# Transformer block with linear attention and eight experts on one core: opening reordered, first transposes moved between the thirds of the running products, expert rows stored by partition with four output buffers

## The chip, the cores and the metric

The kernel runs on one core of one Trainium2 chip, in one launch. A core has a matrix engine (TensorE, PE in the rows), a vector engine (VectorE, DVE), a scalar engine (ScalarE, ACT), a general engine (GpSimd, POOL), a queue engine (SyncE, SP) and 16 DMA engines that all queues share. Each engine executes its own instruction stream in order and waits on semaphores; nothing but these waits ties the engines together. The metric is the device time of one execution in microseconds (us), as the median of three runs.

## The reference

Sixteen sequences of 256 tokens with 128 features (4096 tokens) go through one adaptive-norm block: linear attention with running sums, then a mixture of 8 experts of which each token takes 2.

```python
h = layernorm(x) * (1 + ca) + sa                  # ca, sa, ga, ...: rows made from L0_c @ L0_wmod
q, k, v = split(h @ qkv_w.T + qkv_b)              # 16 heads of 8
q, k = relu(q) + 1e-6, relu(k) + 1e-6
kv    = cumsum(einsum('bhld,bhle->bhlde', k, v), axis=2)
num   = einsum('bhld,bhlde->bhle', q, kv)
den   = maximum(einsum('bhld,bhld->bhl', q, cumsum(k)), 1e-6)
x = x + ga * ((num / den) @ out_w.T + out_b)
h = layernorm(x) * (1 + cb) + sb
# experts: u = rmsnorm(h @ W_in.T); logits = u @ Wr.T; the best 2 of 8 by logits + bias
# oe = rmsnorm((silu(u @ Wg[e].T) * (u @ Wu[e].T)) @ Wd[e].T); out = sum of gates * oe
x = x + gb * (rmsnorm(out) @ W_out.T)
```

## The kernel before

Tokens lie on the 128 partitions, so a sequence ("batch" in the code, `b`) is two tiles (`NT = 2`). The whole program is written out by hand: five functions, one for each engine, each with its own list of instructions and `wait_ge` calls. What stands first in a function is executed first; there is no scheduler. Five stretches follow each other.

**Opening (0 to about 20 us).** SP issues the loads one behind the other on one queue (L385 to L403): modulation weights, the first two batches of `x`, the key/value bias, constants (`cst`), small weights (`small`), output bias `bo`, expert bias, `place`, and the other 14 batches of `x`. The five loads from `cst` to `place` count on one semaphore, `w_ld`, and DVE, POOL and PE wait for all five (`16 * 5`). Then SP waits for `gate_row`, stores it to HBM, reads it back broadcast as `gates_bc` (2 MB), and issues the gate/up weights `wgu` (4 MB), the down weights `wd` (2 MB) and the rest. On POOL the key/value bias is cut into three bf16 parts (L464 to L475), then the gated output bias in the same way (L477 to L483); ACT copies these parts (L573) before its first norm. DVE prepares small weights (L808 to L821) before its first statistics (L829).

**Attention steps (about 17 to 210 us).** `pipelined(eng, step)` calls `step(nrm, qkv, att, prj, inp, rte)` on each engine: in step `s` batch `s` is normalised, batch `s-1` gets q, k and v, batch `s-2` its running sums, `s-3` the output projection, `s-4` the input projection of the experts and `s-5` the routing. Steps 0 to 7 are written out, steps 8 to 15 are a hardware loop of two steps in a pass, steps 16 to 20 are written out again. Within a step:

- POOL forms the products k x v (`kv`, L499, two of 128x1024) once ACT has `k`, and scatters routed rows to HBM (L520).
- PE makes the running sums with a triangular matrix (`running_state`, L1302). For each of the two tiles this is nine matmuls in three thirds (`cc` = 0, 1, 2), each third in a PSUM bank of its own. Before, all three thirds of tile 0 come first in the step, then the transposes of the normalised input (`xn2`, L1347, and `xn`, L1354), the transposes of the reciprocals (L1361), k/v (L1373, L1376), q (L1383), the output projection (L1395, L1398), the thirds of tile 1, and the head sums (L1320 to L1331).
- DVE starts a step with `den` (L1010), multiplies each third by q (L866), and `attnT` (L1035) needs `rdenT` from ACT.
- ACT copies the transposed inputs to `hT` (L610), `h2T` (L616) and `rdenT` (L624), in this order.

Side work is spread over steps: maxima of `wgu` on DVE in steps 2 to 5 (`wmaxs`, L969), squares of `wd` on ACT, one quarter each in steps 4 to 7 (L658), and on POOL the multiplication of `gates_bc` by the output weights (L504, one of 128x2048, in step 2; L511, four of 128x512, one in each of steps 1 to 4).

**Routing tables (210 to 241 us), expert tiles (241 to 415 us).** 39 tiles of 256 rows go through gate, up and down projections; POOL scatters the results to `ybuf` in HBM (L533), two scatters a tile, to the row numbers in `place`.

**End (415 us on).** SP waits for all scatters and loads `ybuf` in four pieces of 2, 2, 4 and 8 batches (`LOADS`, L439). ACT takes the root (`rms_of_rows`, L759), DVE the coefficients (L1200, L1202), POOL multiplies the first expert's rows (`halve`, L547), DVE adds the second (`mix`, L1211), ACT squares, PE transposes and projects (L1530, L1538), DVE adds `x` into an output buffer (`ob`, L1226), and SP stores it (L444). There are two output buffers.

Of the kernel before, what the change touches and what calls it, by code (L numbers as in the profile page):

```python
# [21 lines left out]
ALU = mybir.AluOpType  # L22
ACT = mybir.ActivationFunctionType
AX = mybir.AxisListType

P = 128
# [41 lines left out]
def shape_constants():  # L68
# [14 lines left out]
    token = np.arange(TOK // P)[None, :, None] * P + p[:, None, None]  # L83
    place = (token * K + np.arange(K)).reshape(P, -1).astype(np.uint32)
# [15 lines left out]
def block_kernel(nc, x, c_wmod, weights_all, qkv_b, out_b, e_bias, wguT, wdT, e_norm, consts, place, filler, out):  # L100
    ctx = ExitStack()
    with ctx:
# [114 lines left out]

        spare = prod[0:1].rearrange("o t s -> o (t s)")
# [27 lines left out]
        def in_late(first, n):  # L246
# [18 lines left out]
        half, mix, mixT, ob = (prod[:].rearrange("p t s -> p (t s)")[:, i * 2 * L:(i + 1) * 2 * L].rearrange(  # L265
            "p (j t d) -> p j t d", j=2, t=NT) for i in range(4))
# [13 lines left out]
        LOADS = [(0, 2), (2, 4), (4, 8), (8, B)]  # L280
# [8 lines left out]
        eps_set = sem("eps_set")  # L289
# [22 lines left out]
        scattered, yb_ld, stored = two("scattered"), [sem(f"yb_ld{i}") for i in range(4)], two("stored")  # L312
# [21 lines left out]
        SCALE_STEP = B - WN - 1  # L334
        WO_CHUNKS = 4
# [4 lines left out]
        SQUARE_STEPS = range(B - WN - 4, B - WN)  # L340
# [41 lines left out]
        def _(sp):  # L382
# [16 lines left out]
            sp.dma_start(wgu, wguT).then_inc(wgu_ld, 16)  # L399
# [42 lines left out]
            def store(b, p):  # L442
                sp.wait_ge(ob_done, b + 1)
                sp.dma_start(out[bass.ds(b, 1), :, :].rearrange("o (t p) d -> p (o t) d", p=P),  # L444
                             ob[:, p]).then_inc(stored[p], 16)

            with sp.Fori(0, B // 2) as i:
                for p in range(2):
                    store(2 * i + p, p)
            for p in range(2):  # L450
                sp.wait_ge(stored[p], 16 * (B // 2))
# [3 lines left out]
        def _(pool):  # L455
# [5 lines left out]
            pool.wait_ge(bkv_ld, 16)  # L461
# [1132 lines left out]
```

## Time and profile before

| | us |
|---|---|
| median of 3 runs (lowest, highest) | 454.98 (454.23, 456.43) |
| profiled execution | 456.44 |
| its span in the trace | 454.6 |
| PE, DVE, ACT, POOL busy | 364.9, 337.4, 290.8, 250.6 |

The profiled execution was as long as the longest of the three timed ones; 1.84 us of it lie outside the span. Busy time says little here, since the bound changes from stretch to stretch: between 240 and 410 us PE is busy 166.5 of 170 us, between 120 and 186 us both PE (62.0 of 66) and DVE (58.5) are nearly full, and before 20 us no engine but the DMA is. The rows are read by stretch. In a timeline row the first number is the start from the span's beginning, the second the length from the first to the last instruction of the group, in brackets the idle time of the engine just before it, with what ended it. "issue" means that the trace shows nothing that was waited for.

### The profile page before, as it was taken

The page shows a single profiled execution, that of the slowest core. Times are in us where ns is not written, and L with a number is a line of the kernel's source. Part 1 is how long each engine was busy: PE and PEld are TensorE (multiplying, and loading weights), DVE is VectorE, ACT ScalarE, POOL GpSimd, SP SyncE. Part 2 cuts the span into 40 slices and gives each one's busy share as a digit, 9 for nine tenths or more (in the row PEclk, how much of TensorE's full clock was granted, in tenths as well). Part 3 has the DMA queues.
Part 4 walks back from the last instruction along what each step waited for, and adds up shares of the span by engine and source line. Part 5 has one row for each costly group of instructions (what it writes and reads, how often), then busy time and mean ns, then how long its engine had stood idle before and what let it go on. Part 6 is the DMA issues. An engine that isn't in the chain of part 4 may idle for free.

```text
span 454.6 us, 13206 instructions
## 1 busy us (share of the span) xinstructions
PE 364.9 (80%) x3903; PEld 319.2 (70%) x3904; DVE 337.4 (74%) x1113; ACT 290.8 (64%) x814; POOL 250.6 (55%) x221
## 2 busy tenths in 40 slices
PE   3379999869999999975107999999999999991474
PEld 2158877658888888864105998999999999980353
DVE  3328899657888888867386788789779888790585
ACT  2244687656777777734733778678778778772585
POOL 4359557557777788853630246456546546464331
PEclk9969999998999999997557999999999999996579
DMA  8895000000000000000142122222122222113923
GB/s 238 305 420 218 2 1 25 25 24 20 25 23 28 25 23 23 23 25 25 41 123 68 40 73 65 52 70 64 52 70 64 61 61 71 36 36 89 343 71 92
DMA packets 21907, 35.67 MB, mean 78 GB/s; under 512 B 3827, under 2 KB 17670, under 8 KB 21350
## 3 DMA queue, kind: packets, MB, share of 16 engines
q1 hardware_dynamic: 17206, 25.39, 18.0%
q0 software_dynamic: 4544, 9.39, 6.1%
q10 hardware_dynamic: 128, 0.53, 0.5%
q8 instruction: 15, 0.25, 0.2%
q14 instruction: 14, 0.11, 0.1%
HBM read 23.80 MB, written 13.47 MB: 82 GB/s over the span
## 4 chain that ended last, share of the span: by engine, by line
PE 47%; DVE 22%; issue 13%; DMA 6%; ACT 5%; POOL 4%; DVEq 1%; SPq 1%; another core or an unknown queue 1%; ACTq 0%; POOLq 0%
PE bank L1472 8%; PE bank L1473 7%; PE bank L1474 7%; DVE prod L866 6%; PE bank L1302 4%; PE bank L1489 4%; PE bank L1488 4%; PE bank L1487 4%; PE bank L1458 2%; PE bank L1376 2%; DVE st L829 2%; DVE wmaxs L969 1%; DVE rows L928 1%; DMA out<-prod 1%; DMA place_sb<-place 1%
## 5 line engine op out<-in xcount | busy, mean ns | idle before, releaser
L533 POOL DMA_INDIRECT expert_rows<-late,to_place x78 | 87.5, 1121 | 93.3 <-DVE late L1158 69.7
L499 POOL TENSOR_TENSOR kv<-kv,v 128x1024 f32<-128x1024 f32 x32 | 67.7, 2135 | 40.8 <-ACT kv L634 40.8
L1472 PE MATMUL bank<-late,w_hi 128*128 128x256 f16 x312 | 85.7, 275 | 1.4 <-issue 0.5
L520 POOL DMA_INDIRECT dispatched<-rows,pos x64 | 67.3, 1052 | 34.3 <-issue 17.7
L1473 PE MATMUL bank<-late,w_hi 128*128 128x256 f16 x312 | 85.6, 274 | 0.0
L1474 PE MATMUL bank<-late,w_lo 128*128 128x256 f16 x312 | 85.5, 274 | 0.0
L1302 PE MATMUL bank<-cst,kv 128*128 128x128 f32 x576 | 73.8, 283 | 3.4 <-POOL kv L499 2.5
L1147 DVE SCALAR_TENSOR_TENSOR kv<-bank,uscale,kv 128x512 f32<-128x512 f32 x78 | 58.2, 747 | 21.0 <-ACT kv L714 16.2
L1302 PEld LDWEIGHTS bank<-cst,kv 128*128 128x128 f32 x576 | 69.6, 198 | 4.9 <-POOL kv L499 3.2
L714 ACT ACTIVATE kv<-bank,descale 128x512 f32<-128x512 f32 x78 | 53.5, 685 | 28.3 <-PE bank L1474 27.2
L720 ACT ACTIVATE kv<-kv 128x512 f16<-128x512 f32 x78 | 49.0, 628 | 19.6 <-DVE kv L1147 16.9
L1152 DVE TENSOR_TENSOR kv<-kv 128x512 f16<-128x512 f32 x78 | 53.6, 687 | 6.5 <-issue 3.9
L1487 PE MATMUL bank<-late,kv 128*128 x312 | 54.3, 219 | 0.5 <-DVE kv L1152 0.5
L1488 PE MATMUL bank<-late,kv 128*128 x312 | 54.3, 219 | 0.0
L1489 PE MATMUL bank<-late,kv 128*128 x312 | 54.3, 219 | 0.0
L866 DVE TENSOR_TENSOR prod<-bank,qT 128x384 f32<-128x384 f32 x96 | 50.0, 545 | 5.3 <-PE bank L1302 5.0
L1472 PEld LDWEIGHTS bank<-late,w_hi 128*128 x312 | 30.7, 98 | 6.6 <-issue 3.0
L1474 PEld LDWEIGHTS bank<-late,w_lo 128*128 x312 | 30.7, 99 | 3.7
L1473 PEld LDWEIGHTS bank<-late,w_hi 128*128 x312 | 30.7, 98 | 3.2
L1487 PEld LDWEIGHTS bank<-late,kv 128*128 128x128 f16 x312 | 30.5, 98 | 1.1 <-issue 0.6
L1488 PEld LDWEIGHTS bank<-late,kv 128*128 128x128 f16 x312 | 30.5, 98 | 0.4
L1489 PEld LDWEIGHTS bank<-late,kv 128*128 128x128 f16 x312 | 30.5, 98 | 0.1
(207 smaller groups left out, 790.0 us busy)
## 6 DMA issues: line engine op xcount, KB each, us to landing
late<-dispatched SPq DMA_DIRECT2D x39, 129.0 KB
late<-wguT SPq DMA_DIRECT2D x1, 4096.0 KB, 16.5
late<-expert_rows SPq DMA_DIRECT2D x1, 2064.0 KB, 12.9
gates_bc<-gate_rows SPq DMA_DIRECT2D x1, 2048.0 KB, 6.9
wd<-wdT SPq DMA_DIRECT2D x1, 2048.0 KB, 20.9
out<-prod SPq DMA_DIRECT2D x16, 128.0 KB, 1.8
expert_rows<-late,to_place POOLq DMA_INDIRECT x78
late<-expert_rows SPq DMA_DIRECT2D x2, 516.0 KB, 4.5
```

The lines of the kernel that those rows point to most:

```text
L499: nc.gpsimd.tensor_tensor(kvt[:, 0:HD, :, :], k_in, v_in.to_broadcast([P, HD, H, HD]), ALU.mult).then_inc(kv_done[t], 1)
L520: pool.indirect_dma_start(hbuf, bass.IndirectOffsetOnAxis(ap=pos[:, p, t * K + k:t * K + k + 1], axis=0), rows[:, p, t, k, :], None).then_ ...
L533: pool.indirect_dma_start(ybuf, bass.IndirectOffsetOnAxis(ap=to_place[:, s, r:r + 1], axis=0), yt[:, s, r, :], None).then_inc(y_scat[s], 16)
L866: nc.vector.tensor_tensor(prod[:, t, cc * THIRD * P:(cc + 1) * THIRD * P].rearrange("p (e i) -> p e i", i=P), cum, qT[:, p, t * P:(t + 1) ...
L1147: nc.vector.scalar_tensor_tensor(gu[:, h, :], U[h], uscale[:], sg[:, h, :], ALU.mult, ALU.mult).then_inc(gu_done, 1)
L1302: last = mm(CUM[cc][:, j * P:(j + 1) * P], kv[:, p, t, e * D:(e + 1) * D], tri, start=True, stop=True)
L1472: mm(o, w_hi[:, w], hi, start=True, stop=False)
L1473: mm(o, w_hi[:, w], lo, start=False, stop=False)
L1474: last = mm(o, w_lo[:, w], hi, start=False, stop=True)
L1487: mm(o, gu_hi[:, s % 2, h, g], wd_hi[:, w], start=(f == 0 and r == 0), stop=False)
L1488: mm(o, gu_lo[:, s % 2, h, g], wd_hi[:, w], start=False, stop=False)
L1489: last = mm(o, gu_hi[:, s % 2, h, g], wd_lo[:, w], start=False, stop=(f == FC - 1 and r == RB - 1))
```

## The change

Four groups of edits:

1. **Opening.** `w_ld` counts `cst` and `small` alone (32), `bo` moves to the semaphore of the key/value bias, `ebias` and `place` to that of the last part of `x`. `x` comes in three parts: batches 0 and 1, 2 to 5 (ahead of `ebias` and `place`), 6 to 15 (behind `gates_bc`). `wgu` is issued by ACT behind its first `hT`. DVE does the statistics of batches 0 and 1 and the norm factors of batch 0 first. The first batch takes its k/v bias from the f32 row `bkv` with two one-row f32 matmuls, and does not wait for the bf16 parts. The parts of the gated output bias come behind the first `kv` on POOL, their copies on ACT behind those of batch 1. In step 2 PE does the q, k, v work of batch 1 ahead of the first running sums. POOL's L504 moves out of the steps, to the front of the expert tiles. The squares of `wd` are two quarters each in steps 6 and 7.
2. **Steps.** PE does thirds 0 and 1 of tile 0, then the transposes of the normalised inputs, then third 2.
3. **Expert rows.** `place` numbers the rows by partition: token `n * 128 + p` goes to row pair `p * 32 + n`. Each partition's rows of a load are then contiguous in HBM.
4. **End.** Loads of 1, 3, 4 and 8 batches; the root and the coefficients of the second load come one batch earlier; four output buffers, in the memory of `kv`.

```diff
-    token = np.arange(TOK // P)[None, :, None] * P + p[:, None, None]
-    place = (token * K + np.arange(K)).reshape(P, -1).astype(np.uint32)
+    place = ((p[:, None, None] * (TOK // P) + np.arange(TOK // P)[None, :, None]) * K + np.arange(K)).reshape(
+        P, -1).astype(np.uint32)
...
-        LOADS = [(0, 2), (2, 4), (4, 8), (8, B)]
+        LOADS = [(0, 1), (1, 4), (4, 8), (8, B)]
...
-        SQUARE_STEPS = range(B - WN - 4, B - WN)
+        SQUARE_STEPS = range(B - WN - DN // 2, B - WN)
...
-            sp.dma_start(bo[:], out_b.to_broadcast([P, D])).then_inc(w_ld, 16)
-            sp.dma_start(ebias[:], e_bias.to_broadcast([P, E])).then_inc(w_ld, 16)
-            sp.dma_start(place_sb[:], place).then_inc(w_ld, 16)
-            sp.dma_start(xs[:, 2 * NT:, :], xv[:, 2 * NT:, :]).then_inc(x_rest, 16)
+            sp.dma_start(bo[:], out_b.to_broadcast([P, D])).then_inc(bkv_ld, 16)
+            sp.dma_start(xs[:, 2 * NT:X_MID * NT, :], xv[:, 2 * NT:X_MID * NT, :]).then_inc(x_mid, 16)
+            sp.dma_start(ebias[:], e_bias.to_broadcast([P, E])).then_inc(x_rest, 16)
+            sp.dma_start(place_sb[:], place).then_inc(x_rest, 16)
...
-            sp.dma_start(wgu, wguT).then_inc(wgu_ld, 16)
+            sp.dma_start(xs[:, X_MID * NT:, :], xv[:, X_MID * NT:, :]).then_inc(x_rest, 16)
...
-                sp.dma_start(yb[:, first * NT:end * NT], ybuf[first * L * K:end * L * K, :].rearrange(
-                    "(n p k) w -> p n k w", p=P, k=K)).then_inc(yb_ld[i], 16)
+                sp.dma_start(yb[:, first * NT:end * NT], ybuf[0:TOK * K, :].rearrange(
+                    "(p n k) w -> p n k w", p=P, k=K)[:, first * NT:end * NT]).then_inc(yb_ld[i], 16)
...
-            pool.wait_ge(bkv_ld, 16)
+            pool.wait_ge(bkv_ld, 32)
...
+                    if isinstance(b, int) and b == 0:
+                        out_bias_parts()
...
+                    if isinstance(b, int) and b == 0:
+                        act.dma_start(wgu, wguT).then_inc(wgu_ld, 16)
...
-                if att is not None:
-                    running_state(att, 0, scale)
+                filling = att is not None and first(att[0])
+                if att is not None and not filling:
+                    running_state(att, 0, scale, range(2))
...
                 if inp is not None or qkv is not None:
                     last.then_inc(turn_ps, 1)
+                if att is not None and not filling:
+                    running_state(att, 0, scale, range(2, 3))
...
                     if first(b):
-                        pe.wait_ge(w_ld, 16 * 5)
-                        pe.wait_ge(bias_part, 11)
-                        pe.wait_ge(w_small, 3)
+                        pe.wait_ge(bkv_ld, 32)
+                        for t in range(NT):
+                            mm(KV[:, t * 2 * D:(t + 1) * 2 * D], ones[0:1, :], bkv[0:1, :], start=(t == 0), stop=False)
...
+                if filling:
+                    running_state(att, 0, scale)
...
-                if again(n):
-                    dve.wait_ge(stored[p], 16 * (n - 1))
+                if not (isinstance(b, int) and b < 4):
+                    dve.wait_ge(stored[j % 4], 16 * (i + j // 4))
...
-            coefficients(1)
-            turn_of_batches(0, (2, 3))
+            turn_of_batches(0, (2,))
             coefficients(2)
+            turn_of_batches(0, (3,))
```

PE's list at the opening before, from the modulation matmuls (`sc`, `c_wmod_sb`) to the first running sums (`cst,kv`):

```order
L1265 MATMUL bank<-c_wmod_sb,sc 16x256
L1270 MATMUL bank<-wrn,small 128x8 [waits w_small]
L1354 MATMUL bank<-cst,xn 128x128 [waits xn_done]
L1373 MATMUL bank<-bkv,ones 128x512 [waits bias_part,w_small,w_ld,hT_done]
L1376 MATMUL bank<-small,hT 128x256 x2
L1383 MATMUL bank<-hT,small 128x256
L1302 MATMUL bank<-cst,kv 128x128 [waits gate_done,kv_done_0]
L1302 MATMUL bank<-cst,kv 128x128 x8
L1354 MATMUL bank<-cst,xn 128x128 [waits q_done,xn_done]
```

The same place in the changed kernel, whose line numbers are higher (L1390 is the transpose of `xn`, L1408 the new f32 bias, L1414 the bf16 bias, L1417 and L1424 k/v and q, L1335 the running sums):

```order
L1300 MATMUL bank<-c_wmod_sb,sc 16x256
L1390 MATMUL bank<-cst,xn 128x128 [waits w_ld,xn_done]
L1408 MATMUL bank<-bkv,cst 128x256 [waits bkv_ld,hT_done]
L1417 MATMUL bank<-small,hT 128x256 x2
L1424 MATMUL bank<-hT,small 128x256
L1427 MATMUL bank<-wrn,small 128x8 [waits w_small]
L1390 MATMUL bank<-cst,xn 128x128 [waits q_done,xn_done]
L1414 MATMUL bank<-bkv,ones 128x512 [waits w_small,k_done,bias_part,hT_done]
L1335 MATMUL bank<-cst,kv 128x128 [waits gate_done,kv_done_0]
L1335 MATMUL bank<-cst,kv 128x128 x8
```

The router's matmul (`wrn`) no longer stands ahead of the first transpose, the wait for the bias parts has moved from the first to the second batch, and the running sums that wait for POOL's first `kv` stand behind the whole k, v and q work of the second batch.

PE's list at the start of a step in the loop, before:

```order
L1302 MATMUL bank<-cst,kv 128x128 [waits cum_used_1_0]
L1302 MATMUL bank<-cst,kv 128x128 [waits cum_used_1_1]
L1302 MATMUL bank<-cst,kv 128x128 [waits den_done,cum_used_1_2]
L1302 MATMUL bank<-cst,kv 128x128 x2
L1347 MATMUL bank<-cst,xn 128x128 [waits q_done,xn2_done]
L1354 MATMUL bank<-cst,xn 128x128 [waits q_done,xn_done]
L1354 MATMUL bank<-cst,xn 128x128
L1361 MATMUL bank<-cst,rden 128x128 [waits rden8_done]
L1373 MATMUL bank<-bkv,ones 128x512 [waits k_done,hT_done]
```

The same place in the changed kernel (L1335 the running sums, L1381 and L1390 the transposes, L1399 those of the reciprocals):

```order
L1335 MATMUL bank<-cst,kv 128x128 [waits cum_used_1_0]
L1335 MATMUL bank<-cst,kv 128x128 [waits cum_used_1_1]
L1335 MATMUL bank<-cst,kv 128x128 x2
L1381 MATMUL bank<-cst,xn 128x128 [waits q_done,xn2_done]
L1390 MATMUL bank<-cst,xn 128x128 [waits q_done,xn_done]
L1390 MATMUL bank<-cst,xn 128x128
L1335 MATMUL bank<-cst,kv 128x128 [waits den_done,cum_used_1_2]
L1399 MATMUL bank<-cst,rden 128x128 [waits rden8_done]
L1414 MATMUL bank<-bkv,ones 128x512 [waits k_done,hT_done]
```

The last three of the nine matmuls of tile 0, with their wait for `den`, have moved behind the four transposes. Everything from L1361 on stands as it did.

## Rows read from the trace of the kernel before

**Rows 1.** Busy times by stretch: busy us and (instructions) of each engine, PE clock

```profile
25.00:30.00 5.00, 3.75 (x21) 3.16 (x21) 2.42 (x9) 0.70 (x2) 3.79 (x3) 0.69 0.97 419
120.00:186.00 66.00, 62.01 (x664) 53.34 (x664) 58.48 (x259) 50.63 (x144) 52.77 (x37) 1.00 0.07 24
240.00:410.00 170.00, 166.54 (x2026) 153.14 (x2027) 138.79 (x274) 123.26 (x308) 83.58 (x74) 0.98 0.22 59
```

**Rows 2.** Timeline of the opening, to the start of step 3

```profile
9.48 0.23 DVE L808 TENSOR_SCALAR wrn<-small 128x8 f32<-128x8 f32 x1 [0.81 <-DMA place_sb<-place]
12.12 0.74 POOL L475 TENSOR_TENSOR bkv<-bkv,bkv_part 3x256 bf16<-3x256 bf16 x1
17.23 0.88 ACT L578 ACTIVATE xn<-x_all,nmr,rs 128x128 f32<-128x128 f32 x2 [0.60 <-DVE nmr L846]
20.11 2.08 PE L1376 MATMUL bank<-small,hT 128*128 128x256 f32 x4
23.35 4.21 POOL L499 TENSOR_TENSOR kv<-kv,v 128x1024 f32<-128x1024 f32 x2 [8.05 <-ACT kv L634]
25.53 3.03 PE L1302 MATMUL bank<-cst,kv 128*128 128x128 f32 x18 [2.49 <-POOL kv L499]
35.99 2.33 DVE L969 TENSOR_REDUCE wmaxs<-late 128x1 f32<-128x1024 f32 x2
38.24 0.18 DVE L1010 TENSOR_SCALAR den<-bank 128x32 f32<-128x32 f32 x1
```

**Rows 3.** DMA issues: source and target, queue, count, size, us to landing

```profile
late<-wguT SPq DMA_DIRECT2D x1, 4096.0 KB, 16.5
gates_bc<-gate_rows SPq DMA_DIRECT2D x1, 2048.0 KB, 6.9
small<-weights_all SPq DMA_DIRECT2D x1, 453.5 KB, 5.2
x_all<-x SPq DMA_DIRECT2D x1, 256.0 KB, 3.4
```

**Rows 4.** Timeline of side work in the steps that are written out

```profile
37.66 4.53 POOL L504 TENSOR_TENSOR gates_bc<-gates_bc,woutn 128x2048 f32<-128x2048 f32 x1
77.24 1.04 ACT L658 ACTIVATE w_lo<-wd 128x1024 f16<-128x1024 f32 x1
85.24 0.56 ACT L610 ACTIVATE hT<-bank,mod_cols 128x256 f32<-128x256 f32 x1 [2.90 <-issue]
```

**Rows 5.** Timeline of two steps of the loop, 146 to 160 us, by engine

```profile
146.11 0.42 DVE L1035 TENSOR_TENSOR attnT<-bank,rdenT 128x256 f32<-128x256 f32 x1 [0.66 <-issue]
152.89 2.25 PE L1302 MATMUL bank<-cst,kv 128*128 128x128 f32 x18
154.85 0.29 ACT L603 ACTIVATE sd<-mv,eps_ln 128x2 f32<-128x2 f32 x1
155.71 0.55 DVE L866 TENSOR_TENSOR prod<-bank,qT 128x384 f32<-128x384 f32 x1
155.76 0.56 ACT L610 ACTIVATE hT<-bank,mod_cols 128x256 f32<-128x256 f32 x1 [0.62 <-issue]
156.38 0.38 PE L1373 MATMUL bank<-bkv,ones 3*128 3x512 bf16 x1 [0.58 <-ACT hT L610]
157.09 0.42 DVE L1035 TENSOR_TENSOR attnT<-bank,rdenT 128x256 f32<-128x256 f32 x1 [0.83 <-issue]
159.00 4.23 POOL L499 TENSOR_TENSOR kv<-kv,v 128x1024 f32<-128x1024 f32 x2 [0.98 <-ACT kv L634]
```

**Rows 6.** Timeline of the end, from the loads of the expert rows on

```profile
417.08 2.78 SPq L439 DMA_DIRECT2D late<-expert_rows  x4
421.06 0.31 ACT L759 ACTIVATE rms<-late,eps_rms 128x8 f32<-128x8 f32 x1 [8.08 <-DMA late<-expert_rows]
441.59 0.61 DVE L1226 SCALAR_TENSOR_TENSOR prod<-bank,rinv,x_all 128x128 f32<-128x128 f32 x2 [0.67 <-DMA out<-prod]
451.52 0.61 DVE L1226 SCALAR_TENSOR_TENSOR prod<-bank,rinv,x_all 128x128 f32<-128x128 f32 x2 [0.75 <-DMA out<-prod]
```

More of the change, by code:

```diff
@@ L311, in block_kernel @@
         ln_st, ln2_st = two("ln_st"), sem("ln2_st")
-        scattered, yb_ld, stored = two("scattered"), [sem(f"yb_ld{i}") for i in range(4)], two("stored")
+        scattered, yb_ld, stored = two("scattered"), [sem(f"yb_ld{i}") for i in range(4)], four("stored")
         lr_done, score_done, max_done, idx_done, oh_done = (
@@ L334, in block_kernel @@
         SCALE_STEP = B - WN - 1
+        X_MID = 6
         WO_CHUNKS = 4
@@ L570, in _ @@
             nc.scalar.activation(junk[:, 0:1], eps_ln[:], ACT.Sqrt)
-            act.wait_ge(bo_part, 6)
-            for i in range(3):
-                nc.scalar.activation(bo_ga3[32 * i:32 * i + B, :], bo_ga_part[:, i], ACT.Copy).then_inc(bo_done, 1)
             def norm(b, p, rs_, nmr_, xn_, nm_done, done):
@@ L645, in step @@
                     norm(nrm[0], nrm[1], rs, nmr, xn, ln_nm, xn_done)
+                if qkv is not None and isinstance(qkv[0], int) and qkv[0] == 1:
+                    act.wait_ge(bo_part, 6)
+                    for i in range(3):
+                        nc.scalar.activation(bo_ga3[32 * i:32 * i + B, :], bo_ga_part[:, i],
+                                             ACT.Copy).then_inc(bo_done, 1)
                 if nrm is not None and not isinstance(nrm[0], int):
@@ L1040, in step @@
                     best(rb, rp)
-                if nrm is not None:
+                if nrm is not None and not (isinstance(nb, int) and nb == 0):
                     norm_inv(nb, sd, rs, ln_sd, ln_rs, np_)
@@ L1044, in step @@
                     best_index(rb, rp)
-                if nrm is not None:
+                if nrm is not None and not (isinstance(nb, int) and nb == 0):
                     norm_shift(nb, mv, rs, nmr, ln_rs, ln_nm, np_)
@@ L1233, in _ @@
             mix_experts(*batch_of_turn(0, 0))
+            coefficients(1)
             mix_experts(*batch_of_turn(0, 1))
@@ L1276, in done_by, with running_state @@
                 return min(b, B) if isinstance(b, int) else b
-            def running_state(att, t, scale):
+            def running_state(att, t, scale, chunks=range(3)):
                 b, p, n = att
-                if not scale:
+                if not scale and 0 in chunks:
                     pe.wait_ge(kv_done[t], b + 1)
-                for cc in range(3):
+                for cc in chunks:
                     if t:
@@ L1383, in step @@
                     mm(TB[:, 0:L], wqkv[:, 0:D], hT[:, p, :], start=True, stop=True).then_inc(q_ps, 1)
+                    if first(b):
+                        pe.wait_ge(w_small, 1)
+                        mm(ND[:, 0:E], w_in_rows, wrn[:], start=True, stop=True).then_inc(router_ps, 1)
+                if filling:
+                    running_state(att, 0, scale)
                 if prj is not None:
```

170 lines of the change are left out of this document (97 added, 73 removed).

## The prediction, on record before the result

> **What bounds the kernel now.** I read the busy times by stretch first, then the timeline of each stretch that the change touches, then the list of DMA issues. The reader should see that no single engine is the bound. In the 66 us of loop steps PE is busy 62.0 us and DVE 58.5 [rows 1]; both have short gaps. Over the expert tiles PE is busy 166.5 of 170 us [rows 1]; the change leaves their instructions alone, so these 170 us stay. That leaves three places: the opening, the start of every step, and the end.
>
> In the opening the first normalised input is ready late: DVE waits until 9.48 for the landing of `place`, which it doesn't use there, ACT's first `xn` comes at 17.23, k/v at 20.11, POOL's first `kv` at 23.35, and step 3 starts with `den` at 38.24 [rows 2]. In a loop step (`attnT` at 146.11 and 157.09: 10.98 us) the same gap shows on three engines: ACT idles 0.62 before `hT`, PE 0.58 behind it, DVE 0.83 (0.66 in the step before) ahead of `attnT` [rows 5]. At the end ACT waits for the first expert rows until 421.06, 3.98 us behind the issue, and DVE waits for stores [rows 6].
>
> **Opening, part by part.** `small` lands 5.2 us behind its issue at 2.5, so at 7.7; the first `x` took 3.4 us, so about 4.6 [rows 3]. DVE's statistics of both batches then run 4.7 to 6.2, and ACT's `xn` (0.88, [rows 2]) is done by about 7.8. Two transposes bring 8.5, `hT` 9.1. The two f32 bias matmuls are not in the trace. Each has the shape of the k/v matmuls, of which two (four passes) took 2.08 us [rows 2]: with that, 2.1 us; a bound below is the bf16 form in [rows 5], 0.38. I take 2.1, since an f32 row is nearest to the f32 rows. So k/v ends at 9.2 + 2.1 + 2.1 = 13.4 where it ended at 22.2. POOL is now later: it waits for `bo` too (about 8.1) and ran 8.0 us of bias work from 4.82, of which 1.27 was waiting; so it is free at about 15.0, and `kv` starts at 15.0 where it started at 23.35. That bounds the saving on this chain at 8.3 us. Batch 1 follows on PE: transposes at 16.4, k/v and q done at 21.3, running sums behind them (3.03 and about 2.6, head sums 2.2) to about 29.2. Before, PE was through at 37.6, just ahead of `den` at 38.24 [rows 2]: 8.4 us saved.
>
> What is late next is `wgu`. In step 2 DVE needs it for two maxima of 2.33 us together, just ahead of `den` [rows 2]. It took 16.5 us behind `gates_bc`, 6.9 us [rows 3]. Now ACT issues it at about 9.2, ahead of `gates_bc` (about 12.5). The DMA moved 419 GB/s at 25 to 30 us [rows 1]. Up to 12.5 `wgu` gets about 1.1 of its 4.2 MB. If both then share evenly, `gates_bc` (2.1 MB) lands at about 22.7 and `wgu`, with the last part of `x` beside it, at 28 to 30. If nothing were gained it would be 32.7 as before; alone it would be done at about 20. I take 29: maxima until 31.4, `den` at 31.4 instead of 38.24, so **6.8 us saved** in place of 8.4; bounds 3.1 (landing at 32.7) and 9.5 (PE reaches its higher clock earlier than it did, and `wgu` is there by 26). POOL has `gates_bc` to wait for between `kv` of batch 0 and 1. Queued behind this wait is `kv` of batch 1, which PE needs at 29.2; it would hurt only if `gates_bc` landed later than about 25.8.
>
> The page "DMA: Bandwidth & Descriptors" of the Trainium skill (sections on queues and rings, and on issuing engines) says that an engine takes turns between the queues it has work for, and that issuing from several engines saves issue time only. By that rule the second queue for `wgu` adds no bandwidth, and the landing times are the shared ones of my sum rather than the 20 us; no row before shows two such loads at once.
>
> The bias parts, the f32 row of the first batch, and the output bias copies lie on engines that wait at that time; I cost them at nothing beyond the times above. Squares of `wd`: a quarter costs ACT 1.04 us and 0.19 for its sum [rows 4]. Steps 4 and 5 lose one each; in step 4 it was on the path for about 0.4, in step 5 the maxima on DVE end last. Steps 6 and 7 get 1.23 more each; ACT waited about 0.5 and 0.9 there for DVE, so 0.3 to 0.8 shows. Behind step 6 ACT stood still for 2.90 us with nothing shown [rows 4], which may hide it or not: **-0.3**, bounds -1.5 and +0.5.
>
> POOL's L504 (4.53 us, [rows 4]) now runs at about 241 to 246, where POOL idled until its first scatter at 254.7: nothing. In step 2 it hid behind ACT's k.
>
> The page "SBUF — State Buffer" (on the engine doors) says that VectorE and GpSimd take turns on one port pair for whole instructions, when VectorE reads two operands there or copies in its fast mode. By it DVE's small copy of row numbers would wait for L504 and the first tile of the experts would come about 0.8 us later. The trace doesn't bear this out: L504 ran beside DVE's `den` at 38.24 without delay, though that reads PSUM.
>
> **Loop steps.** A third of `running_state` is three matmuls, 2.25 / 3 = 0.75 us [rows 5]. The transposes come that much earlier. `hT` was issued at 155.76; it can start when ACT is through with `sd`, 154.85 + 0.29 = 155.1. So 0.62 is gained of the 0.75. PE idled 0.58 for it, and that is all PE has to give: from then on PE is the bound of the step. DVE's `attnT` has 0.66 and 0.83 to give. Third 2 comes 0.4 later, at about 155.5; DVE's last product of tile 0 reads it at 155.71 at the earliest: 0.2 to spare. POOL idles 0.98 a step and keeps 0.4. So each full step becomes 10.4 us. Eight loop steps and step 16: 9 x 0.58 = **5.2 us**. Bounds: 0 if third 2 or another wait takes the place, 7.5 if the two-sided gap goes wholly. In steps 3 to 7 `hT` follows right behind `sd` or the maxima bound: nothing.
>
> **End.** First load 264 KB in runs of 2 KB instead of 516 KB in runs of 1 KB: 3.98 us before, 3.4 for 256 KB in the busy opening [rows 3], 1.8 for 128 KB stores. I take 2.7: 1.3 saved (0.6 to 2.1). The second coefficients, needed one batch earlier, cost and save about alike, 0.5 saved. Four buffers take away DVE's waits for stores, 0.67 and 0.75 [rows 6] and one of like size between them, 2.0 together; I take 1.6, since PE and ACT are close behind. Sum **3.4 us**, bounds 1 and 6. The scatters now write 516-byte rows 33 KB apart for neighbouring tokens; only the last one is on the path (2.4 us), and I see no cost.
>
> **Sum.** 6.8 - 0.3 + 5.2 + 3.4 = 15.1 us. Against the profiled execution's 456.44 that is 441.3. The median of the runs is 1.46 below the profiled one, so 439.9; I say **440.0 us**.
>
> **Rivals.**
>
> *`wgu` is no earlier* (0.17). It lands at 32.7 as before, the opening saves 3.1: 443.7 us. For it: the DMA was at its full rate from 16 us on. Against: it was idle or slow from 12 to 16.
>
> *The gap in the loop moves instead of going* (0.13). DVE's third product or POOL's `kv` ends last: no 5.2, 445.2 us. Against: the spare 0.2 and 0.4.
>
> *More than I sum* (0.17). PE's clock rises early in the opening, the 2.90 us standstill of [rows 4] goes, stores and loads at the end gain their upper bounds: 4 to 6 us more, about 435.
>
> *Slower* (0.02). One mechanism: PE, with no idle time left in the loop, is granted its lower level (1.2 GHz). In the 25 to 30 stretch at 0.69 of full speed the same 18 matmuls took 3.03 us instead of 2.25 [rows 1, 2], k/v 2.08; a step of 10.4 us of PE work would take at least 14. From about five such steps on (3.6 us each against 15.1, with the rest kept) the kernel is slower than before; with all eight it takes 469. Against it: 0.98 to 1.00 granted at 94 to 98% busy [rows 1].
>
> My own case has 0.51, with a range of 437 to 443. What a measurement of this kernel can tell from no change is about 0.5%, 2.3 us. Faster by more than that: all of the first four cases but a rest of 0.02 in which several lower bounds meet: 0.96. Same 0.02, slower 0.02. The range for 8 in 10 takes in the first two rivals and part of the third: 435 to 446.
>
> **What would show it.** `xn` of batch 0 near 7 us and k/v by 14; `kv` on POOL near 15; the first maxima waiting for `wgu` and ending near 31; `den` of step 3 near 31.4. In the loop, steps of 10.4 us, no idle of PE ahead of the k/v bias, `attnT` right behind DVE's product. At the end the first root 2.7 us behind the load's issue, and no wait of DVE for a store. Wrong would be: loop steps of 11 us; `den` of step 3 later than 35; PE clock below 0.95 in the loop; expert tiles longer than before.

## The result, and the profile after

The changed kernel takes 439.86 us (median of four runs, 437.86 to 440.80), beside 455.71 for the kernel before (454.23 to 458.97): a ratio of 0.964, interval 0.957 to 0.970. 440.0 was forecast. The profiled execution took 440.27 us, its span 438.4 us, 16.2 less than before; 15.1 were forecast for it.

The span splits as follows (us). The rows of a step are taken from its `den` to the next one's:

| stretch | before | after | difference |
|---|---|---|---|
| start to `den` of step 3 | 38.24 | 28.90 | -9.3 |
| step 3 | 10.32 | 12.62 | +2.3 |
| steps 4, 5, 6 | 32.06 | 31.22 | -0.8 |
| steps 7 and 8 | 28.58 | 25.82 | -2.8 |
| steps 9 to 16 | 87.56 | 83.39 | -4.2 |
| step 17 | 12.05 | 13.19 | +1.1 |
| from there to the loads of the expert rows | 208.27 | 208.39 | +0.1 |
| loads to the end of the span | 37.5 | 34.9 | -2.6 |

The timeline of the opening of the changed kernel, which answers to [rows 2] (start, length, engine, line, in brackets the idle time ahead and what ended it):

```profile
6.48 0.88 ACT L585 ACTIVATE xn<-x_all,nmr,rs 128x128 f32<-128x128 f32 x2 [0.73 <-DVE nmr L830]
9.39 2.07 PE L1408 MATMUL bank<-bkv,cst 1*128 1x256 f32 x4 [0.72 <-ACT hT L617]
11.39 2.07 PE L1417 MATMUL bank<-small,hT 128*128 128x256 f32 x4
15.59 4.20 POOL L506 TENSOR_TENSOR kv<-kv,v 128x1024 f32<-128x1024 f32 x2
20.96 5.18 PE L1335 MATMUL bank<-cst,kv 128*128 128x128 f32 x36
26.01 1.29 POOL L515 TENSOR_TENSOR gates_bc<-gates_bc,small 128x512 f32<-128x512 f32 x1 [3.78 <-DMA gates_bc<-gate_rows]
26.65 2.33 DVE L993 TENSOR_REDUCE wmaxs<-late 128x1 f32<-128x1024 f32 x2
27.24 4.21 POOL L506 TENSOR_TENSOR kv<-kv,v 128x1024 f32<-128x1024 f32 x2
28.90 0.18 DVE L1034 TENSOR_SCALAR den<-bank 128x32 f32<-128x32 f32 x1
29.43 2.56 PE L1335 MATMUL bank<-cst,kv 128*128 128x128 f32 x12 [1.01 <-POOL kv L506]
```

`xn`, k/v (done at 13.5) and POOL's first `kv` (15.59) are where the prediction put them, and the f32 bias row took 2.07 us. The maxima of `wgu` (L993) follow without a wait. POOL is the one that waits: until 26.01 for `gates_bc`, with `kv` of batch 1 queued behind it at 27.24, and PE stands 1.01 us for that. The 12 matmuls behind this wait take 2.56 us; in [rows 5] 18 took 2.25. The DMA issues, against [rows 3]:

```profile
late<-wguT ACTq DMA_DIRECT2D x1, 4096.0 KB, 15.8
gates_bc<-gate_rows SPq DMA_DIRECT2D x1, 2048.0 KB, 15.1
```

`gates_bc` takes 15.1 us instead of 6.9. A step of the loop, against [rows 5], and the end, against [rows 6]:

```profile
131.44 0.83 PE L1335 MATMUL bank<-cst,kv 128*128 128x128 f32 x6
131.58 0.29 ACT L610 ACTIVATE sd<-mv,eps_ln 128x2 f32<-128x2 f32 x1
131.79 0.57 ACT L617 ACTIVATE hT<-bank,mod_cols 128x256 f32<-128x256 f32 x1
132.42 0.39 PE L1414 MATMUL bank<-bkv,ones 3*128 3x512 bf16 x1
133.12 0.42 DVE L1068 TENSOR_TENSOR attnT<-bank,rdenT 128x256 f32<-128x256 f32 x1
...
143.59 0.42 DVE L1068 TENSOR_TENSOR attnT<-bank,rdenT 128x256 f32<-128x256 f32 x1
...
403.53 1.76 SPq L442 DMA_DIRECT2D late<-expert_rows  x4
406.10 0.30 ACT L774 ACTIVATE rms<-late,eps_rms 128x4 f32<-128x4 f32 x1 [6.43 <-DMA late<-expert_rows]
...
435.37 0.61 DVE L1260 SCALAR_TENSOR_TENSOR kv<-bank,rinv,x_all 128x128 f32<-128x128 f32 x2 [0.47 <-PE bank L1584]
```

The third `cc` = 2 (131.44) runs while ACT makes `hT`; none of these rows has a bracket, on any of the three engines; the step is 10.47 us instead of 10.98. At the end the first root comes 2.57 us behind the issue, and no add waits for a store. Busy times in the loop, against [rows 1]:

```profile
120.00:186.00 66.00, 63.42 (x679) 54.92 (x677) 58.62 (x258) 50.73 (x146) 54.83 (x40) 1.00 0.08 27
```

PE is busy 63.4 of 66 us (62.0 before) at a granted clock of 1.00: no sign of the rival in which it falls to its lower level.

One pair of rows was not in the sum. It lies where the experts start; the first row is the copy in the kernel before:

```profile
242.69 0.16 DVE L1140 COPY to_place<-late 128x2 uint32<-128x2 uint32 x1
...
227.73 4.50 POOL L534 TENSOR_TENSOR gates_bc<-gates_bc,woutn 128x2048 f32<-128x2048 f32 x1 [6.66 <-DVE late L1148]
228.35 3.90 DVE L1173 COPY to_place<-late 128x2 uint32<-128x2 uint32 x1
```

DVE's copy of row numbers (two for each partition) takes 3.90 us (before: 0.16). It ends at 232.25, POOL's instruction at 232.23.

### The profile page after: what moved, and what is told of

It is laid out like the page before. It is cut to its first block, busy times and chain, and to the rows that moved or that the text cites. A ratio compares the mean times of both kernels' runs of the same rounds, so it can differ in the third digit from the quotient of the medians.

```text
span 438.4 us, 13203 instructions
## 1 busy us (share of the span) xinstructions
PE 366.1 (84%) x3906; PEld 321.1 (73%) x3907; DVE 338.8 (77%) x1113; ACT 290.9 (66%) x814; POOL 249.9 (57%) x221
## 3 DMA queue, kind: packets, MB, share of 16 engines
HBM read 23.80 MB, written 13.47 MB: 85 GB/s over the span
## 4 chain that ended last, share of the span: by engine, by line
PE 56%; DVE 19%; issue 10%; DMA 7%; ACT 3%; POOL 3%; DVEq 1%; another core or an unknown queue 0%; ACTq 0%; SPq 0%; POOLq 0%
PE bank L1518 8%; PE bank L1520 8%; PE bank L1519 8%; PE bank L1335 6%; DVE prod L890 5%; PE bank L1533 4%; PE bank L1535 4%; PE bank L1534 4%; DMA gates_bc<-gate_rows 3%; PE bank L1504 2%; PE bank L1417 2%; DVE st L813 2%; PE bank L1444 1%; ACT junk L782 1%; DVE x_all L1085 1%
## 5 line engine op out<-in xcount | busy, mean ns | idle before, releaser
L1335 PE MATMUL bank<-cst,kv 128*128 128x128 f32 x576 | 77.0, 286 | 1.2 <-POOL kv L506 1.0
L1335 PEld LDWEIGHTS bank<-cst,kv 128*128 128x128 f32 x576 | 72.0, 201 | 1.9 <-POOL kv L506 1.1
L585 ACT ACTIVATE xn<-x_all,nmr,rs 128x128 f32<-128x128 f32 (+1 forms) x64 | 28.0, 485 | 6.5 <-DVE nmr L830 5.7
L1533 PEld LDWEIGHTS bank<-late,kv 128*128 128x128 f16 x312 | 30.5, 98 | 1.9 <-issue 1.4
L1534 PEld LDWEIGHTS bank<-late,kv 128*128 128x128 f16 x312 | 30.5, 98 | 0.4
## 6 DMA issues: line engine op xcount, KB each, us to landing
late<-wguT ACTq DMA_DIRECT2D x1, 4096.0 KB, 15.8
gates_bc<-gate_rows SPq DMA_DIRECT2D x1, 2048.0 KB, 15.1
```

The costliest lines, as they stand in the source:

```text
L1335: last = mm(CUM[cc][:, j * P:(j + 1) * P], kv[:, p, t, e * D:(e + 1) * D], tri, start=True, stop=True)
L1533: mm(o, gu_hi[:, s % 2, h, g], wd_hi[:, w], start=(f == 0 and r == 0), stop=False)
L1534: mm(o, gu_lo[:, s % 2, h, g], wd_hi[:, w], start=False, stop=False)
```

## Experiments

Twelve more runs were made, in three groups of four; each group had a chip of its own. The kernel before took 456.74 us in the first group, 458.22 in the second and 448.07 in the third, so times are compared within a group and by their ratio to it. `after_again` is the changed kernel as it is, `thirds_only` the kernel before with one edit, `both_pool` the changed kernel with two; the others are the changed kernel with one. The changed kernel itself ran in group 2 only, so in the other two groups its edits are judged by their siblings. A time expected in us was meant for the first chip and isn't to be held against another one: the steps and waits are.

| group | kernel | us | ratio (interval) |
|---|---|---|---|
| 1 | thirds_undone | 445.31 | 0.977 (0.971, 0.983) |
| 1 | wgb_early | 437.69 | 0.958 (0.953, 0.963) |
| 1 | chunk_behind | 434.37 | 0.951 (0.945, 0.957) |
| 1 | written10 | 435.74 | 0.953 (0.947, 0.958) |
| 2 | after_again | 439.02 | 0.962 (0.954, 0.970) |
| 2 | wgu_sp | 439.57 | 0.961 (0.954, 0.969) |
| 2 | squares_old | 440.59 | 0.964 (0.955, 0.972) |
| 2 | by_token | 438.66 | 0.959 (0.949, 0.968) |
| 3 | loads_old | 433.34 | 0.967 (0.964, 0.969) |
| 3 | ob2 | 435.98 | 0.974 (0.970, 0.978) |
| 3 | thirds_only | 441.61 | 0.985 (0.982, 0.989) |
| 3 | both_pool | 430.38 | 0.959 (0.956, 0.962) |

### The transposes between the thirds: undone, and alone

`thirds_undone`:

```diff
-                    running_state(att, 0, scale, range(2))
+                    running_state(att, 0, scale)
...
-                if att is not None and not filling:
-                    running_state(att, 0, scale, range(2, 3))
```

> The changed kernel with all three thirds of tile 0 ahead of the transposes again, in every step but step 2, which stays as changed. My theory (the gap behind the late transposes was PE's own idle time, 0.52 a step): loop steps go from 10.46 back to 10.97 us, PE idles 0.58 ahead of the k/v bias, about 5 us slower over eight loop steps and step 16, and 1 to 2 us more in steps 3 to 7 if the same gap was there: 445 us. Rival (the loop gained from elsewhere, from the moved side work for instance): loop steps stay near 10.5 us and the kernel near 440.

The loop steps are 10.97 us again (10.37 to 10.40 in the three other kernels of the group), and the gap is back as it was. Two rows of its timeline:

```profile
145.28 0.56 ACT L617 ACTIVATE hT<-bank,mod_cols 128x256 f32<-128x256 f32 x1 [0.61 <-issue]
145.90 0.38 PE L1412 MATMUL bank<-bkv,ones 3*128 3x512 bf16 x1 [0.58 <-ACT hT L617]
```

The other way round, `thirds_only` puts the same edit alone into the kernel before.

> The kernel before with the one edit that the transposes stand between the thirds of the running products in steps 3 to 16, all else as before. Theory: loop steps 10.4 to 10.5 us instead of 10.97 as in the changed kernel, and 0.2 to 1.2 us less in steps 3 to 7: 5 to 6 us faster than before, 450 us. It also gives a second trace of steps 7 and 8 of the old kernel (13.47 and 15.11 us in the first): if they are near 13.5 and 13 here, the fast step 8 of the changed kernel is no gain of the change. Rival (the gain in the loop hangs on the other edits, side work among them): 455.

0.985 of 448.07 is 6.6 us less (5.1 to 8.1). Its loop steps are 10.30 us, as in the three changed kernels of its group. Taken away, the edit costs 0.57 to 0.60 us a step on one chip (10.97 against 10.37 to 10.40). Put in alone it leaves the same step as all edits together, and that is 0.67 us below the 10.97 of the first trace; no trace of the kernel before was taken on this chip, so part of the 0.67 can be the chip's. The rival that the gain needs the other edits has fallen. And steps 7 and 8 took 11.13 and 10.54 us in it, with the old opening and the old squares.

### Steps 7 and 8: is the gain there one of the change?

`written10` writes out steps 8 and 9 too, so that the hardware loop begins with step 10.

> The changed kernel with steps 8 and 9 written out too, so that the hardware loop begins with step 10. The two slow steps 7 and 8 (12.2 and 13.6 us from den to den in the changed kernel, 13.5 and 15.1 before; 10.46 in the loop) show ACT, DVE and PE all standing still by issue or remote. Theory A (it comes with entering the loop, the code of its first pass): the slow steps become 9 and 10, steps 7 and 8 take about 10.5. Theory B (it comes with the work of steps 7 and 8, the first scatters among it): they stay 7 and 8. Either way about 440 us.

Step 7 took 12.20 and step 8 12.19 us, step 9 10.14, and the first two of the loop 10.39 and 10.40. Theory A is refuted: the slow steps did not move with the loop. Theory B is not shown by this run alone. The changed kernel a second time:

> The changed kernel once more, for a second trace. In its first trace two written-out steps took longer than in three kernels that keep them as they are: step 8 took 13.58 us (12.30, 12.19 and 11.64 in the others) and the step behind the loop 13.19 (10.97 to 10.99). If these standstills are chance, this trace has them smaller or elsewhere, near 12.2 and 11.0, and the kernel takes 437 to 438.5 in it. If they belong to this kernel, both come back: 13.6, 13.2 and 440.

Step 17 came back at 11.03, step 8 at 12.94, between the two expectations. The place stays, the size varies. Steps 7, 8 and 17, in us:

| | step 7 | step 8 | step 17 |
|---|---|---|---|
| before | 13.47 | 15.11 | 12.05 |
| changed, first trace | 12.24 | 13.58 | 13.19 |
| after_again | 12.44 | 12.94 | 11.03 |
| chunk_behind (group 1) | 12.25 | 12.30 | 10.97 |
| squares_old (group 2) | 13.48 | 13.06 | 11.59 |
| thirds_only, loads_old, ob2, both_pool (group 3) | 11.13 | 10.53 to 10.54 | 10.40 to 10.41 |

In group 3 the standstills are absent in all four kernels, with the old opening or the new. No edit is needed for them to come or go, and the -2.8 and +1.1 us in the first table can't be credited to the change. One thing stays open: where the standstills occur, step 7 took 13.47 and 13.48 us in the two traces with the old squares (before, `squares_old`) and 12.20 to 12.99 in the eight with the new ones, so the place of the squares may have a part in 1 us of step 7. What makes the engines stand still was not found.

### The opening: wgu, and POOL's order

`wgu_sp` issues `wgu` on SP again, behind `gates_bc`:

```diff
-                        act.dma_start(wgu, wguT).then_inc(wgu_ld, 16)
...
+            sp.dma_start(wgu, wguT).then_inc(wgu_ld, 16)
             sp.dma_start(xs[:, X_MID * NT:, :], ...
```

> The changed kernel with the gate/up weights wgu issued on SP's queue again, behind gates_bc, and not by ACT at the first hT. Theory: gates_bc has the DMA for itself again and lands about 7 us behind its issue, near 18 instead of 26, so kv of batch 1 is not held up on POOL; but wgu lands near 31 to 33 instead of 24.6, the maxima on DVE wait for it, and den of step 3 comes at 33.5 to 35 instead of 28.9. Against the changed kernel: step 3 then loses 2.3 to 2.7 us less; 2 to 3.5 us slower in all, 441 to 443.5. Rival (wgu lands no later, DMA shares nothing): den of step 3 near 29 and the kernel about 2.5 us faster, 437.

Its DMA issues, and the wait of the maxima in its timeline:

```profile
late<-wguT SPq DMA_DIRECT2D x1, 4096.0 KB, 16.6
gates_bc<-gate_rows SPq DMA_DIRECT2D x1, 2048.0 KB, 7.2
```

```profile
28.40 2.35 DVE L992 TENSOR_REDUCE wmaxs<-late 128x1 f32<-128x1024 f32 x2 [2.11 <-DMA late<-wguT]
30.66 0.18 DVE L1033 TENSOR_SCALAR den<-bank 128x32 f32<-128x32 f32 x1
```

Both theories missed. `den` of step 3 comes at 30.66, not 33.5, and step 3 takes 9.92 us instead of 10.93; step 4 begins at 40.58, in `after_again` at 40.63. The queue of `wgu` makes no difference to the start of step 4: what one of two loads gains, the other loses. `wgu` lands at 28.4 here (issue at 11.79), at 24.6 in the changed kernel and at about 32.7 before. By the rows, the 4.3 us between here and before are the store of the gates: it was issued at the same time (8.70 and 8.71) and took 7.0 us with the last 14 batches of `x` ahead of it, 2.7 with only four of them there.

`chunk_behind` turns POOL's order. `kv` of batch 1 comes first, then the piece that waits for `gates_bc`:

```diff
-                    if isinstance(b, int) and b < WO_CHUNKS:
-                        if b == 0:
+                    for c in ((), (0, 1), (2,), (3,))[b] if isinstance(b, int) and b < WO_CHUNKS else ():
+                        if c == 0:
                             pool.wait_ge(gates_in, 16)
```

> The changed kernel with the first piece of the output weights (the POOL instruction that waits for gates_bc) behind kv of batch 1 instead of ahead of it. My theory: in the changed kernel kv of batch 1 started at 27.2 because POOL stood until gates_bc landed at 26.0, and PE waited 1.0 us for it at 29.4, then ran at its lower clock until about 33.6 (12 matmuls in 2.56 us instead of 1.58). With the order turned PE doesn't wait: step 3 comes 1.0 us sooner, and 2.3 us if the clock does not fall: 437.6 to 439. Rival: the clock falls anyway, and the wait at 29.4 is replaced by one for another load or for DVE: 440.

The timeline, in the same place as above:

```profile
22.50 4.21 POOL L506 TENSOR_TENSOR kv<-kv,v 128x1024 f32<-128x1024 f32 x2
26.86 2.52 POOL L515 TENSOR_TENSOR gates_bc<-gates_bc,small 128x512 f32<-128x512 f32 x2 [0.16 <-DMA gates_bc<-gate_rows]
29.47 1.58 PE L1335 MATMUL bank<-cst,kv 128*128 128x128 f32 x12
```

PE doesn't wait, the 12 matmuls take 1.58 us, and step 3 takes 9.92. On the same chip the kernel is 3.3 us faster than `wgb_early`, which has the wait (its step 3: 12.84) and differs from it in the place of L534 too. At the start of step 4 it is 2.1 us ahead (40.02 against 42.10), and 1.8 ahead of `written10`. That is less than the 2.9 between their steps 3, since `den` came 0.8 later in it (30.10 against 29.26). Of the 2.1 us, 0.5 are there when PE begins the 12 matmuls (29.47 against 30.01); the other 1.5 come behind, where PE runs slower in `wgb_early`. Of the time below the expected 437.6 to 439, steps 8 and 17 have 3.5 us (12.30 and 10.97 against 13.58 and 13.19 in the first trace), which is not shown to be the edit's. Busy times from 29 to 35 us, PE first, the granted clock third from the end, of the changed kernel, `after_again` and `chunk_behind`:

```profile
29.00:35.00 6.00, 5.57 (x28) 5.08 (x29) 3.82 (x16) 1.67 (x4) 3.69 (x3) 0.72 1.02 405
```

```profile
29.00:35.00 6.00, 5.06 (x36) 4.32 (x37) 4.52 (x17) 2.37 (x7) 4.44 (x3) 1.00 1.04 399
```

```profile
29.00:35.00 6.00, 5.96 (x45) 5.22 (x45) 5.13 (x19) 2.87 (x8) 0.57 (x2) 1.00 1.05 396
```

PE waited 1.01 us for `kv` in the first, and 0.94 in the second, whose step 3 took 10.93. 0.72 is a mean over six us in part at 1.2 GHz, the lower level. Nine traces have this wait. In four of them PE had waited 0.62 to 0.94 us, the clock was 1.00 and step 3 took 10.6 to 11.1 us; in five it had waited 1.01 to 1.84 us, the clock was 0.58 to 0.72 and step 3 took 12.6 to 14.7. No run sets the length of the wait by itself, so that the wait brings the lower level is read from this order, not tested. And its length alone doesn't decide: `wgu_sp` has a longer wait of PE in the same step, for `den`, and kept its clock.

```profile
30.99 0.91 PE L1334 MATMUL bank<-cst,kv 128*128 128x128 f32 x6 [1.36 <-DVE den L1033]
```

```profile
29.00:35.00 6.00, 4.06 (x26) 3.08 (x25) 5.35 (x18) 2.20 (x7) 0.59 (x1) 1.00 1.07 374
```

This wait stands behind the 12 matmuls, the others stand ahead of them. What is shown without a rival is that in `chunk_behind` and `both_pool`, where PE doesn't wait at all, the granted clock stays at 1.00.

### POOL's long multiplication

`wgb_early` puts L534 back into step 2.

> The changed kernel with POOL's multiplication of gates_bc by the output weights (4.5 us) back in step 2, between kv of batch 1 and the second piece of the output weights. My theory now (against my prediction): it holds up DVE's copy of row numbers at the start of the experts, 3.90 us long in the changed kernel where it took 0.16 before, and so costs 0.8 us there. The copy is 0.16 us again, the first expert tiles come 0.8 us earlier. In step 2 and 3 POOL is then later: kv of batch 2 is not needed before 36 us, POOL is free at about 37.2, so up to 1 us is lost there: 439 to 440.5 in all. Rival (the long copy is an artefact of the trace or has another cause): the first expert tiles do not move, 440 to 441.

```profile
224.05 0.16 DVE L1174 COPY to_place<-late 128x2 uint32<-128x2 uint32 x1
```

The copy takes 0.16 us again. In the ten traces that have L534 at the start of the experts it takes 3.19 to 3.96 us, and ends 0.02 to 0.03 us behind L534 in each. But nothing is won there: from the first transposes of the experts to ACT's last `kv` (gate) it takes 166.1 us in `wgb_early`, 165.3 in `chunk_behind` of the same chip, which has the long copy. The 0.8 us the other way lie in the first tile, where PE's clock was still low in `wgb_early` (0.75 granted from 226 to 230 us, 0.99 in `chunk_behind`); from the transposes of the second tile on it is 160.1 and 160.0. The mechanism holds, its price doesn't show; the 439 to 440.5 us forecast missed, and the kernel's lower time lies in steps 8 and 17.

### The squares, the layout, the loads, the buffers

`squares_old`:

```diff
-        SQUARE_STEPS = range(B - WN - DN // 2, B - WN)
+        SQUARE_STEPS = range(B - WN - 4, B - WN)
```

(and one quarter in a step.)

> The changed kernel with the squares of wd back in four steps, one quarter each in steps 4 to 7. My term for the move was -0.3 us (a gain of 0.3 to 1.5 for the old place at one end, a loss of 0.5 at the other). In this trace steps 4 and 5 should grow by up to 0.4 each and steps 6 and 7 shrink by up to 0.8 together: 439.5 to 440.5, not to be told from the changed kernel by its time. Rival (the moved squares filled standstills): step 7 shrinks by over 1 us, 438.5.

Step 4 takes 10.41 us instead of 9.92, steps 5 and 6 the same. Step 7 took 13.48, but with the old squares it took 11.13 in `thirds_only`, the same as with the new ones in that group. The move saved 0.5 us in step 4 and cost nothing later.

`by_token` restores the order of the rows in `place` and in the loads.

> The changed kernel with the expert rows in HBM in the order of the tokens again, so that a load is written in runs of 1 KB and a scatter's rows lie 1 KB apart for neighbouring tokens. Two things may show. At the end: the first load (one batch) takes longer than 2.57 us, about 3.2, the later ones by 5 to 15%, 0.6 to 1.2 us lost. Over the expert tiles: 36 tiles took 144.14 us before and 144.6 in all kernels with rows by partition. Theory: that 0.5 us is the scatters' wider spread, and is 144.1 here; rival: it has nothing to do with the layout and stays 144.6. In all 440 to 441 by the first, 440.5 to 441.5 by the second.

The first root comes 2.83 us behind the issue (2.57 and 2.68 with rows by partition), and from the issue to the last add it takes 32.0 us, as with them (31.8, 32.1). The layout is worth 0.2 us at the start of the end and nothing at its end. It did show in the last load: 12.6 us in the order of the tokens, 10.7 to 11.3 with rows by partition, but nothing waited for it. The expert tiles are 0.6 us longer in the changed kernel's trace than before, which the prediction had named as a sign of being wrong. That did not come from the layout or from any other edit: from the transposes of the second tile to ACT's last `kv` (gate) it takes 160.1 us in the first trace of the changed kernel and in `by_token`, and 159.6 in the kernel before and in all four kernels of group 3, the changed ones and `thirds_only`.

`loads_old` restores `LOADS` and the places of the roots and coefficients:

```diff
-        LOADS = [(0, 1), (1, 4), (4, 8), (8, B)]
+        LOADS = [(0, 2), (2, 4), (4, 8), (8, B)]
...
             mix_experts(*batch_of_turn(0, 0))
-            coefficients(1)
```

> The changed kernel with the loads of the expert rows in pieces of 2, 2, 4, 8 batches and with the second coefficients one batch later, as before; rows by partition and four output buffers stay. My terms: first root 1.3 us later (2.6 us behind the issue with one batch, 3.98 before; with rows by partition about 3.5 to 3.9 for two), the order of the coefficients 0.5. From the issue of the loads to the last add: 31.8 to 32.1 us in the changed kernel, 33.1 to 33.8 here, and 1.3 to 1.8 us slower in all. Rival (a later stage is the bound of the end, so the earlier start is lost): 32.0 to 32.5, no more than 0.5 us.

```profile
398.74 1.76 SPq L442 DMA_DIRECT2D late<-expert_rows  x4
402.72 0.31 ACT L774 ACTIVATE rms<-late,eps_rms 128x8 f32<-128x8 f32 x1 [8.34 <-DMA late<-expert_rows]
...
431.59 0.61 DVE L1258 SCALAR_TENSOR_TENSOR kv<-bank,rinv,x_all 128x128 f32<-128x128 f32 x2 [0.45 <-DVE rinv L1249]
```

The root stands 3.98 us behind the issue, as in [rows 6] to the hundredth, though the rows lie by partition here. The end takes 32.85 us, 0.7 to 1.1 more than the changed kernel's 31.8 to 32.1: between the two expectations. The comparison crosses chips. On the same chip `both_pool`, with the new loads, takes 32.72, but the granted clock fell there once more (0.59 from 21 to 24 us behind the issue; 1.00 in `loads_old` and `after_again`), so it can't decide. Of the 1.4 us by which the first root comes sooner, the first add keeps 0.4 (it stands 9.8 us behind the issue instead of 10.2).

`ob2` goes back to two output buffers.

> The changed kernel with two output buffers again, in the same place as the four. My term: four buffers save 1.6 us of the 2.0 us that DVE waits for stores. So waits of 0.6 to 0.75 us for the output's DMA are back on DVE, and from the issue of the loads to the last add it takes 33.4 to 33.7 us instead of 31.8 to 32.1. Rival (PE and ACT are just behind, the waits only move): 32.0 to 32.5.

```profile
425.48 0.61 DVE L1260 SCALAR_TENSOR_TENSOR kv<-bank,rinv,x_all 128x128 f32<-128x128 f32 x2 [0.19 <-DMA out<-kv]
426.76 0.61 DVE L1260 SCALAR_TENSOR_TENSOR kv<-bank,rinv,x_all 128x128 f32<-128x128 f32 x2 [0.60 <-DMA out<-kv]
428.19 0.61 DVE L1260 SCALAR_TENSOR_TENSOR kv<-bank,rinv,x_all 128x128 f32<-128x128 f32 x2 [0.75 <-DMA out<-kv]
```

Its end takes 33.3 us, 1.2 to 1.5 more than with four buffers (31.8 to 32.1, on other chips); the waits are back.

### Both of POOL's edits together

`both_pool` has the order of `chunk_behind`, and L534 behind the pieces in step 2.

> The changed kernel with both of POOL's orders put right: the first piece of the output weights behind kv of batch 1, and the multiplication of gates_bc by the output weights right behind it in step 2. POOL is then free at about 34 us, and kv of batch 2 is needed at 34.8. Expected: step 3 at 9.9 us as with the first edit alone (10.9 to 12.6 in the changed kernel), DVE's first copy of row numbers 0.16 us long. The second edit adds 0.1 to 0.3 us to the first: 434 us, 0.950 to 0.955 of before. Rival (POOL's 4.5 us in step 3 hold up DVE's products, which read two operands in SBUF or PSUM, as the copy was held up): step 3 above 11 us and 436 or more.

```profile
22.43 4.21 POOL L506 TENSOR_TENSOR kv<-kv,v 128x1024 f32<-128x1024 f32 x2
26.61 2.51 POOL L515 TENSOR_TENSOR gates_bc<-gates_bc,small 128x512 f32<-128x512 f32 x2
29.09 4.52 POOL L520 TENSOR_TENSOR gates_bc<-gates_bc,woutn 128x2048 f32<-128x2048 f32 x1
34.65 4.24 POOL L506 TENSOR_TENSOR kv<-kv,v 128x1024 f32<-128x1024 f32 x2 [1.03 <-ACT kv L644]
...
219.00 0.16 DVE L1174 COPY to_place<-late 128x2 uint32<-128x2 uint32 x1
```

POOL ends 1 us before it is needed, step 3 takes 9.92 us, the copy 0.16. At 430.38 us this is the lowest time measured, on the quickest chip; its ratio (0.959) is below those of its group, but missed the 0.950 to 0.955 expected. By ratio alone it is not told from the changed kernel's 0.964 and 0.962, whose denominators contain the standstills of steps 7 and 8, and the changed kernel itself did not run in that group. What is shown is that the edit of POOL's order takes away PE's wait, and leaves its clock at 1.00, in each of the two kernels that have it.

## Why the prediction was right, step by step

- **Start to step 4: 6.8 us forecast, 7.0 measured** (48.56 to 41.52). The size is right and the step named as late next is wrong. The sum had `gates_bc` landing at 22.7 and `wgu` at 28 to 30. They landed at about 25.9 and 24.6 (issue at 10.81 and 8.79), so the maxima didn't wait and `den` came at 28.90. The step that failed is the even share: 4 MB took 15.8 us and 2 MB beside them 15.1, so `wgu` moved at about twice the rate of `gates_bc`. The condition under which POOL's wait would hurt (a landing later than 25.8) was met by 0.1 us. `den` gained 9.3 us, and step 3 took 12.6 where 9.9 is to be had: 1.0 of wait, and about 1.7 of PE's work at the lower level. Step 4 began 1.5 to 1.7 us later than in the two kernels with POOL's order turned (41.52 against 40.02 and 39.86, on other chips). No run takes the opening's edits apart one by one; as a group they bring `den` of step 3 from 38.08 (`thirds_only`) to 29.3 to 30.6 on the chip of group 3. The estimate of the f32 row (2.1, measured 2.07) held. That the two loads share the DMA, as the page "DMA: Bandwidth & Descriptors" of the Trainium skill has it (section on issuing engines: they are not separate queues), agrees with the rows: 6.9 and 7.2 us alone, 15.1 beside `wgu`.
- **Squares: a loss of 0.3 forecast, a gain of 0.5 measured.** The loss forecast for steps 6 and 7 did not occur. Step 6 is the same in `squares_old` and `after_again` (9.74 and 9.75), so the quarter added there was not on the path. The transposes, forecast at nothing in steps 3 to 7, brought another 0.3 in steps 4 and 5 (10.41 in `thirds_only` against 10.65, 11.45 against 11.55).
- **L504 moved: nothing forecast, nothing to be seen, for the wrong reason.** The prediction said that the trace doesn't bear out the port rule of the page "SBUF — State Buffer" (section "SBUF: two separate sides": VectorE, in its fast copy, and GpSimd hold one port pair by turns, each for its whole instruction). It does: the copy ends with POOL's instruction in all ten traces where the two meet. The row used against the rule, `den` at 38.24, reads PSUM, and so could not speak against it (the prediction said as much, and still left the rule out). So the engines are tied by more than their waits on semaphores. The 0.8 us that the prediction worked out for this case did not show: from the second tile's transposes on, the kernels with the long copy and without it take the same.
- **Loop: 5.2 us forecast, 4.7 measured**: 4.2 over steps 9 to 16, and 0.5 put down for step 8 like the others, which its standstill hides. That is 0.52 a step where 0.58 was forecast; PE has a small new wait elsewhere (row below). The mechanism was right in the rows shown: the third moved behind the transposes, the gap went on ACT, PE and DVE, and undoing the edit brought it back.

```profile
138.57 0.43 PE L1353 MATMUL bank<-qT,s 128*32 128x128 f32 x8 [0.24 <-DVE prod L890]
```

- **Steps 7, 8 and 17: 1.2 us less beside that 0.5, not in the sum and not shown to be the change's.** Without them the span would be 15.0 us shorter. This is the 2.90 us standstill of [rows 4], which the prediction's third rival wanted to see go: it does go, on some chips, in old and new kernels alike.
- **End: 3.4 us forecast, 2.6 measured.** The buffers gave 1.2 to 1.5 (1.6 forecast), loads and coefficients together 0.7 to 1.1 (1.8 forecast): the first load's 1.3 us came at the root (1.4 measured) but were not worth that at the end, since only 0.4 reached the first add.

The terms as measured sum to 7.0 + 0.5 + 0.3 + 4.7 + 2.6 - 0.1 (from step 18 to the loads) = 15.0 us, against 15.1. That is partly luck: 1.3 us too much for the loop and the end stands against 1.3 too little for the opening, the squares and the transposes. The other 1.2 us of the trace's 16.2 lie in the steps with the standstills: chance, as far as is shown. So 439.86 beside the forecast 440.0 is closer than the working behind it.

## What to carry to other kernels

Order the instructions of an in-order engine by need, and ask of each wait what is queued behind it: here POOL's wait for a load whose product PE used at 35.4 us held up one that PE used at 28.4, and with the lower clock behind it cost 1.5 to 2.1 us by the start of step 4. A load that is moved to run beside another takes its time from that one, so name the consumer of both. And a gain in one trace counts only if a second trace of the same kernel repeats it, or if undoing the edit takes it away, best on the same chip.

## What the runs showed of the hardware that was not expected

PE's clock: in the opening the same work was granted 1.00 in four traces and 0.58 to 0.72 in five, and a wait of PE of a few tenths more lay ahead of the lower ones (1.01 to 1.84 us against 0.62 to 0.94), while a wait of 1.36 us behind the next 12 matmuls left it at 1.00. A VectorE copy of 1 KB took 3.19 to 3.96 us while GpSimd multiplied, and 0.16 otherwise. A 2 MB load from HBM took 12.6 to 12.9 us in runs of 1 KB and 10.7 to 11.3 with each partition's rows in one run. Three chips differ by 2% on the same kernel (448.07 to 458.22 us), and the loop steps by 1 to 2% (10.30, 10.37 to 10.40 and 10.47 us with the edit).
